# Middle stage of a graph network on one core: three steps of the variance move from VectorE to ScalarE and GpSimd, and the order of VectorE's steps changes

## The reference

```
mean = s / safe_deg
mean_sq = segment_sum(e * e) / safe_deg
var = relu(mean_sq - mean * mean)
std = sqrt(var + EPS)
agg = concatenate([mean, mx, mn, std])           # 512 per node
h = concatenate([x, agg, agg * amp, agg * att])  # 13 * 128 per node
h = relu(h @ W_post1 + b_post1) @ W_post2 + b_post2 + x
x1 = layernorm(x + h)
```

## Time and profile before

| | |
|---|---|
| measured time, median of 3 | 8026.22 us (8023.64 to 8038.06) |
| profiled execution, own time as the page gives it: its span | 5758.1 us |
| instructions | 177079 |
| PE busy in the span | 5133.3 us (89%) |
| DVE busy | 4769.9 us (83%) |
| ACT busy | 2880.2 us (50%) |
| POOL busy | 3892.4 us (68%) |
| `phase_n1` in the span | about 2280 to 2482 us |

### The profile page before, as it was taken

The page is one execution under the profiler, slowest core; times in us unless marked ns, Lnnn a source line. Parts: engine busy times, 40 slices in busy tenths (PEclk is TensorE's granted clock), DMA queues, the critical chain, the costliest instruction groups (busy, mean ns, idle before and its releaser), DMA issues. The chain is left out here.

```text
span 5758.1 us, 177079 instructions
## 1 busy us (share of the span) xinstructions
PE 5133.3 (89%) x42482; PEld 4048.9 (70%) x42482; DVE 4769.9 (83%) x12692; ACT 2880.2 (50%) x6715; POOL 3892.4 (68%) x3977
## 2 busy tenths in 40 slices
PE   3999999999999997969888876999999999999993
PEld 2888888888888886438777754666666666666663
DVE  4999999999999997767777766888888888888887
ACT  1556666565665654123333334555555555555556
POOL 2777777777777774037777744777777777777772
PEclk7999999999999999968898977999999999999996
DMA  6666666666666664322222212222222222222221
GB/s 155 160 160 157 159 156 157 158 157 157 157 158 157 156 157 127 96 58 54 54 54 54 54 33 45 53 53 53 53 53 54 53 53 53 53 53 53 53 53 48
DMA packets 667245, 544.72 MB, mean 95 GB/s; under 512 B 365794, under 2 KB 544171, under 8 KB 666853
## 3 DMA queue, kind: packets, MB, share of 16 engines
q0 software_dynamic: 126336, 262.13, 19.2%
q1 hardware_dynamic: 415050, 163.69, 12.3%
q10 hardware_dynamic: 125724, 117.57, 8.0%
HBM read 517.22 MB, written 25.61 MB: 94 GB/s over the span
## 5 line engine op out<-in xcount | busy, mean ns | idle before, releaser
L1780 POOL DMA_INDIRECT Gt<-TAB,metat x1632 | 1597.5, 979 | 617.0 <-issue 496.1
L565 POOL DMA_INDIRECT G<-Atab,ms x1616 | 1573.1, 973 | 578.9 <-issue 461.5
L1268 POOL DMA_INDIRECT Gc<-XS,metac x672 | 644.6, 959 | 241.5 <-issue 190.5
L1820 DVE SCALAR_TENSOR_TENSOR M<-neqt,Gt 128x256 f32<-128x256 f32 x816 | 310.7, 422 | 312.3 <-DMA Gt<-TAB,metat 312.3
L669 ACT COPY BS<-BK 128x512 f32<-128x512 f32 x808 | 465.5, 576 | 198.5 <-PE BK L758 191.0
L1413 ACT COPY acc<-CP 128x300 f32<-128x300 f32 x630 | 269.5, 428 | 554.3 <-PE CP L1451 546.3
L612 DVE TENSOR_TENSOR_SCAN ST<-mm,ST,ET 128x512 f32<-128x512 bf16 x404 | 516.3, 1278 | 0.2
L614 DVE TENSOR_TENSOR_SCAN ST<-mm,ST,ET 128x512 f32<-128x512 bf16 x404 | 506.6, 1254 | 0.0
L758 PE MATMUL BK<-ident,ST 128*128 128x128 f32 x3232 | 485.0, 273 | 1.9 <-ACT BS L669 1.9
L1984 PE MATMUL SR<-P,Gt 128*128 128x128 f32 x3264 | 473.5, 288 | 0.0
L1984 PEld LDWEIGHTS SR<-P,Gt 128*128 128x128 f32 x3264 | 395.7, 191 | 70.2 <-issue 70.2
(11 more groups left out here) (291 smaller groups left out, 11642.8 us busy)
## 6 DMA issues: line engine op xcount, KB each, us to landing
mm<-MM ACTq DMA_DIRECT2D x404, 256.0 KB
ZR<-in_eft SPq DMA_DIRECT2D x404, 128.0 KB
dstb<-DF SPq DMA_DIRECT2D x404, 128.0 KB
Gt<-TAB,metat POOLq DMA_INDIRECT x1632
G<-Atab,ms POOLq DMA_INDIRECT x1616
ad<-ADT SPq DMA_DIRECT2D x816, 0.2 KB
WB<-Btab SPq DMA_DIRECT2D x404, 32.0 KB
Gc<-XS,metac POOLq DMA_INDIRECT x672
```

The lines of the kernel that those rows point to most:

```text
L565: e.indirect_dma_start(G[:, k, s, :], None, Atab, bass.IndirectOffsetOnAxis(ap=ms[:, k, s:s + 1], axis=0)).then_inc(l_g[k], 16)
L1268: e.indirect_dma_start(G[:, k, s, :], None, XS, bass.IndirectOffsetOnAxis(ap=meta[:, k, s:s + 1], axis=0)).then_inc(l_g[k], 16)
L1780: e.indirect_dma_start(G[:, k, s, :], None, TAB, bass.IndirectOffsetOnAxis(ap=meta[:, k, s:s + 1], axis=0)).then_inc(l_g[k], 16)
```

## The change

`a(g)` is split. Its first product, the mean, becomes `averages(g)`, the first step in DVE's iteration. The product of the sum of squares with 1/degree goes to POOL (`squares`), the square of the mean to ACT (`squared`). The difference and max(.,0)+EPS stay on DVE as `variance(g)`, the last step of the iteration. The scaling of `x1` by `dinv` goes from DVE's f2 to ACT (`scaled`), which raises a new semaphore `s_xs`; PE's s and SP's store wait for it. POOL may run two groups ahead of DVE's variance.

```diff
@@ tiles and semaphores
+        sr = sbt(ph, "sr1", [128, 2, 512])
+        s_mn = sem("n_mn")
+        s_ms = sem("n_ms")
+        s_sr = sem("n_sr")
+        s_xs = sem("n_xs")
@@ SP, store(g)
                 e.wait_ge(s_f2, g + 1)
+                e.wait_ge(s_xs, g + 1)
@@ DVE
-            def a(g):
+            def averages(g):
                 c, n, _ = cols(g)
-                q = g % 2
-                t = lambda k: tmp[:, k, 0:n]
-                r = dq[:, g % 3, 0, 0:n]
-                ch.sync()
                 e.wait_ge(n_q[g % 3], 16 * (g // 3 + 1))
                 if g >= 2:
                     e.wait_ge(s_b, g - 1)
-                ch(e.tensor_tensor(mean[:, q, 0:n], acc[:, 0, c], r, ALU.mult))
-                ch(e.tensor_tensor(t(0), acc[:, 1, c], r, ALU.mult))
-                ch.sync()
-                ch(e.tensor_tensor(t(1), mean[:, q, 0:n], mean[:, q, 0:n], ALU.mult))
-                ch.sync()
-                ch(e.tensor_tensor(t(0), t(0), t(1), ALU.subtract))
-                ch.sync()
-                ch(e.tensor_scalar(std[:, q, 0:n], t(0), 0.0, EPS, ALU.max, ALU.add))
+                e.tensor_tensor(mean[:, g % 2, 0:n], acc[:, 0, c], dq[:, g % 3, 0, 0:n], ALU.mult).then_inc(s_mn, 1)
+
+            def variance(g):
+                _, n, _ = cols(g)
+                q = g % 2
+                e.wait_ge(s_ms, g + 1)
+                e.wait_ge(s_sr, g + 1)
+                ch(e.tensor_tensor(sr[:, q, 0:n], sr[:, q, 0:n], tmp[:, q, 0:n], ALU.subtract))
+                ch.sync()
+                ch(e.tensor_scalar(std[:, q, 0:n], sr[:, q, 0:n], 0.0, EPS, ALU.max, ALU.add))
                 ch.raises(s_var)
@@ DVE, f2(g)
-                ch.sync()
-                for b in range(nb):
-                    o = c.start // 128 + b
-                    ch(e.tensor_scalar(acc[:, 0, o * 128:(o + 1) * 128], x1[:, q, b, :], dinv[:, o:o + 1], None, ALU.mult))
                 ch.raises(s_f2)
 
-            steps(NG, [(1, a2), (2, dd), (3, ee), (4, f1), (5, f2), (0, a)])
+            steps(NG, [(0, averages), (1, a2), (2, dd), (3, ee), (4, f1), (5, f2), (0, variance)])
+
+        @blk.gpsimd
+        def _(e):
+            def squares(g):
+                c, n, _ = cols(g)
+                e.wait_ge(n_q[g % 3], 16 * (g // 3 + 1))
+                if g >= 2:
+                    e.wait_ge(s_var, g - 1)
+                e.tensor_tensor(sr[:, g % 2, 0:n], acc[:, 1, c], dq[:, g % 3, 0, 0:n], ALU.mult).then_inc(s_sr, 1)
+
+            steps(NG, [(0, squares)])
@@ ACT
+            def squared(g):
+                _, n, _ = cols(g)
+                e.wait_ge(s_mn, g + 1)
+                if g >= 2:
+                    e.wait_ge(s_var, g - 1)
+                e.activation(tmp[:, g % 2, 0:n], mean[:, g % 2, 0:n], ACT.Square).then_inc(s_ms, 1)
+
+            def scaled(g):
+                c, n, nb = cols(g)
+                e.wait_ge(s_f2, g + 1)
+                for b in range(nb):
+                    o = c.start // 128 + b
+                    m = e.activation(acc[:, 0, o * 128:(o + 1) * 128], x1[:, g % 2, b, :], ACT.Identity,
+                                     scale=dinv[:, o:o + 1])
+                m.then_inc(s_xs, 1)
...
-            steps(NG, [(2, h), (4, rs), (6, k), (0, roots)])
+            e.wait_ge(s_dv, 2)
+            steps(NG, [(0, squared), (2, h), (4, rs), (6, k), (5, scaled), (0, roots)])
@@ PE, s(g)
-                e.wait_ge(s_f2, g + 1)
+                e.wait_ge(s_xs, g + 1)
```

## The result

The kernel after the change takes 8059.82 us (median of 10 runs, 8031.14 to 8077.09), the kernel before in the same comparison 8011.19 us (10 runs, 7977.31 to 8038.06). The ratio is 1.006, 95% interval 1.0041 to 1.0079: slower by 33 to 63 us. The medians differ by 48.6 us. The forecast was slower by 36.7 us, 8063 us.

What follows compares the result with a forecast made beforehand. PE paces the changed stage before; afterwards a loop through dq's landing does. Seven turns +33.7, ahead of them +3.7, behind -0.7 give +36.7 us on 8026.2, so 8063 us; range 8044 to 8078.

Steps and rivals of the forecast that it cites:

- PE sets the pace before: Changed stage: PE paces each group at 12.89 us, so taking work from DVE or ACT gains nothing while PE never waits.
- The loop from dq's landing: Changed stage: averages at DVE's head waits for dq, whose load waits for f2; turn 17.91 us against PE's 12.89.
- hold by POOL: In the loop: POOL's product blocks one two-SBUF-input DVE instruction, 1.01 us a group; ends 0 and 1.43.
- seven turns: Head of iteration 5 to that of 12: loop rules, 123.5 us against 89.8 before, excess +33.7 us.
- tail: b(11) to the stage's end: PE, then a DVE chain as before, 40 us; change -0.7 us, ends -2.7 and +1.
- ahead of group 5: Stage start, before the loop rules: b(0) to b(3) start later by 1.5, 1.5, 0.5, 0.2; sum +3.7 us.
- Rival A: Loop without POOL's hold: turn 16.90 us, +28.3 us, 8054 us; chance 0.17.
- rival B: Idle PE returns at half clock: 8065 to 8067 us, or at least 8113 if low throughout; chance 0.20.
- Outside the stage: Whole kernel: 2268.1 us between span and median lies outside first and last instruction, taken as unchanged.
- waits of averages: Sign of being right: averages on DVE waits for dq's DMA in seven or eight groups, some 4 us each.
- rival C: dq arrives in time and PE keeps the pace: +3 to +8 us, 8031 us; chance 0.10.
- rival D: ACT's Square needs another table than Sqrt: 1.28 us a load, up to 0.3 a turn, +2; no separate chance.

Runs made afterwards that it cites:

- e1: Changed kernel with the mean back at the end of DVE's iteration and ACT's square late in its list: stage 181.87 us, ratio to the kernel before 1.0017.
- e2: Changed kernel with SP's store one iteration later, so loads no longer stand behind it: stage 189.00 us, ratio to the kernel before 1.0008.
- e4: Kernel before with only the mean moved to the head of DVE's iteration: stage 211.90 us, ratio 1.0041, on 5751.69 us.
- e3: Changed kernel with POOL's product made to wait for DVE's a2 of the group before: stage 212.63 us.
- e6: Changed kernel with the scaling by dinv back on DVE behind f2: stage 218.55 us, turns 17.29 us.
- e0: Kernel before, unedited, profiled a second time: stage 183.23 us, span 7987.9 us.
- e5: Changed kernel with SP issuing dq ahead of xt from group 6 on: stage 218.61 us.

## Why the prediction was right, step by step

**PE sets the pace before, so freeing DVE gains nothing.** Right: in e1, with 2.3 us a group gone from DVE, a group still takes 12.89 us.

**The loop from dq's landing over f2 and SP's queue to the next landing.** Right, and shown twice: e2 cuts it at SP and 31 of the 36.7 us go, e4 makes it with nothing else of the change. Its terms, forecast and measured in the turn shown above:

| term | forecast | measured |
|---|---|---|
| mean, to a2's start | 0.69 | 0.61 |
| a2 to dd, with the hold by POOL | 1.74 | 1.80 |
| dd to the end of f2 | 6.73 | 6.73 |
| hop, scaling on ACT, hop | 1.30 | 1.44 |
| X1D to dq | 1.57 | 1.57 |
| issue of dq to the mean | 5.88 | 5.61 |
| turn | 17.91 | 17.76 |

The errors are small and of both signs. The sum for the stage hit to a tenth because the error of the seven turns and of the tail (-2.2 together) and that ahead of group 5 (+2.1) cancelled: luck, not precision. It is luck too that the time came within 4 us of 8063: the kernel before took 8011.19 us beside it, not the 8026.22 that the sum started from, so that the measured difference is 48.6 us, with 36.7 inside its interval.

Of the 1.8 us in the turns, 1.1 lie in the first, which took 16.77 us: dq(5) landed while DVE still waited for PE, POOL's product was over before a2 began, and nothing was held.

```profile
3423.92 1.27 POOL L1043 TENSOR_TENSOR sr<-acc,dq 128x512 f32<-128x512 f32 x1 [11.73 <-DMA dq<-DQ]
...
3426.31 0.68 DVE L982 SCALAR_TENSOR_TENSOR std<-acc,std 128x512 f32<-128x512 f32 x1
```

I had charged the hold in seven turns; it fell in six, and e3 gives back just these six. The next five turns take 17.53 to 17.98 us, 17.73 in the mean. The last takes 16.35 where the forecast had 16.0, as mean(12) waited for PE, not for dq.

**The hold by POOL, 1.01 us from the last stage.** Right: 1.07 us (1.76 for 0.69), and e3 removes it. The Trainium skill's rule (SBUF — State Buffer, Who interferes with whom) fits this too: a2 with two SBUF inputs was held by POOL, the products of dd with one PSUM input were not (0.69 and 0.68 with POOL beside them, in e3). Rival A is out, but for the first turn, which was one without a hold.

**Ahead of group 5, +3.7.** Too small: +5.8. Two things were left out. b(0) started 1.5 later as said, but then ran slower: from its start to DVE's next step it took 14.0 us (3372.82 to 3386.84) against 12.95 before. And for b(2) and b(3) I had PE covered by y, r and s from the moment b ends; but DVE sees b's end 0.27 us after y has begun on PE (3399.52 to 3399.79), and a2 starts only from there. Every group of this stretch is 12.95 us, against 11.16, 12.01 and 12.46 before, which makes 1.8, 0.9 and 0.5 for the 1.5, 0.5 and 0.2 I had; and e2 shows the same 12.95 with all of y, r and s ahead of b.

**The clock, rival B.** Its mechanism happens and is hidden in the turn, as worked out: the idle PE comes back at half clock, and b's first matmuls show it in this timeline of the changed kernel.

```profile
3498.26 2.04 PE L1154 MATMUL PP<-mean,w 128*128 128x512 f32 x2 [3.04 <-issue]
3500.10 3.62 PE L1154 MATMUL PP<-acc,w 128*128 128x512 f32 x4
...
3504.71 1.02 PE L1154 MATMUL PP<-mean,w 128*128 128x512 f32 x2
```

Two matmuls take 2.04 us and later 1.02, the granted clock being 0.50 from 3498.30 to 3503.30 and 1.00 from 3504.70 to 3512.00. From b's start to y it takes 12.8 to 14.2 us in five of the six turns after the first, for 11.16 at full clock: 1.7 to 3.0 lost, where I had supposed 2. In the other one, with 1.57 us of idle time ahead of it, b is not slowed (11.24). b then ends later, PE idles 1.6 to 4.7 us, 3.2 in the mean and not 5, and its busy share is 83%, not under the 80% I had named. In the turn from 3495.74, y begins at 3512.43, 0.95 us ahead of the next mean at 3513.38, and y, r and s end at 3514.33, still ahead of the end of a2 at 3515.75. In the last turn the slow b(10) did decide: DVE had its end at 3547.45, dq(12) some 0.2 us before. b(11) does not start slow: mean(12) came right behind b(10), so nothing shows in the tail.

**Outside the stage.** Here a reading was wrong, though no term hung on it: I took the 2268 us between median and span as time outside the first and last instruction. The spans of the later profiles are within 2.2 us of the times of their executions; the first profile belonged to the lower level of the whole. It did no harm because the sum was a difference inside one stage.

**Smaller readings and signs.** The waits of averages were to be some 4 us each in seven or eight groups; they are 7.1 to 7.6 us in the six that wait for dq in the loop. The prediction's own loop would have given it: 17.91 us less some 10.3 of DVE's work leave about 7.6 (an estimate from its terms). The stage of 242 us rests on a length of 205 us, where its marks, 2280 and 2482, are 202 apart. And in the earlier trace rows the slow and the fast four matmuls stand in neighbouring groups, each behind 1.9 us of idle time, not 2 to 3; PE's idle time before the groups of that layer goes from 0.4 to 3.3 us, so these rows alone did not show which idle time brings the lower clock.

**Not slower, rival C.** Out: the landing would have had to be 0.8 us, it is 5.6.

**A table load, rival D.** Out: ACT loads no table between the first mean and the end of the stage. Its two loads (1.28 us each) come before, at 3352.42 and 3357.45, as they do in the kernel before.

## What to carry to other kernels

When a step moves to the head of an in-order engine's iteration, follow what it reads back through the queue that loads it: here one DMA queue put each load behind a store that needed the end of the same iteration, and 5.6 us of slack turned into a loop through DVE, ACT, SP and the DMA. A loop of that kind is summed from landing to landing, and it is broken at the cheapest link, here one digit in SP's order, rather than by making the engines in it faster. Where the pacing engine has no idle time, work moved off another engine is worth nothing (12.89 us a group with it and without), and a step that lies on the loop pays for its hops as well (0.45 us a turn, e6).

## What the runs showed of the hardware that was not expected

The same program ran at two levels. Timeline groups of POOL's largest line, in e0 (span 7987.9 us) and e4 (span 5768.6 us), the columns being busy us, mean ns, idle before and what ended it:

```profile
L565 POOL DMA_INDIRECT G<-Atab,ms x1616 | 1696.2, 1050 | 1514.6 <-DVE EE L591 798.3 <-issue 644.2 <-DMA ms<-in_meta 72.1
```
```profile
L565 POOL DMA_INDIRECT G<-Atab,ms x1616 | 1587.0, 982 | 566.5 <-issue 474.9 <-DMA ms<-in_meta 78.8 <-DVE EE L591 12.8
```

POOL issues the same gathers in 982 or 1050 ns each, but stands idle 1514.6 us before them at the upper level, 798.3 of it until DVE's EE, against 566.5. The mean granted clock is 0.844 there and 0.947 here. Which of these is the cause is open. All runs of e4 to e6 were on one chip and at the lower level, all other experiments on three other chips and at the upper, so the chip may be the cause as well; no run tries it. The stage without gathers is the same at both levels (183.23 and 183.30 us), and jobs at the lower level agree within 11 us among 8 runs of the kernel before, those at the upper within 50 to 61 in each comparison (10 to 19 runs).

A dq of 768 KB issued 0.6 us sooner behind the stores, and ahead of xt, landed only some 0.2 us sooner behind X1D's issue in the median (e5).
